# Gathers of 125 edge rows in place of 128 in a three-hop graph kernel

## The reference

```python
edge_index = jnp.stack([src, dst])
h = jnp.maximum(_layernorm(x, axis=-1), 0.0)
head = edge_index[0]; tail = edge_index[1]
rel = edge_emb[edge_type]
agg = entity_emb                      # h
out = jnp.zeros_like(entity_emb)
for _ in range(3):
    h = agg[head]
    t = agg[tail]
    left = h @ q_w
    right = jnp.tanh(rel * t @ k_w)
    att = jnp.sum(left * right, axis=1)
    w = softmax of att over the edges of one head
    msg = w[:, None] * rel * t
    summed = jax.ops.segment_sum(msg, head, num_segments=n)
    agg = summed / jnp.maximum(cnt, 1.0)[:, None]
    norm = jnp.linalg.norm(agg, axis=1, keepdims=True)
    agg = agg / jnp.maximum(norm, 1e-12)
    out = out + agg + entity_emb
x = x + out
```

## Time and profile before

| | |
|---|---|
| median of 3 runs | 2142.53 us |
| lowest, highest | 2138.31, 2146.28 us |
| the profiled execution | 2145.74 us |
| its span, first to last instruction | 2144.0 us |
| POOL, DVE, PE, ACT busy | 1240.4, 1280.6, 1106.5, 843.2 us |
| packets on POOL's DMA queue (q0) | 38400, 72.99 MB |
| packets on SP's DMA queue (q1) | 160708, 228.35 MB |
| TensorE clock granted, mean | 0.684 of full speed |

### The profile page before, as it was taken

One profiled execution on the slowest core, in us unless ns is written; L12 is line 12 of the kernel. 1 busy time (PEld: TensorE's weight loads), 2 busy tenths in 40 slices (PEclk: granted clock), 3 DMA queues, 4 the chain that ended last, 5 costly groups with the idle time before them and its releaser, 6 DMA issues. The chain is left out here.

```text
span 2144.0 us, 22842 instructions
## 1 busy us (share of the span) xinstructions
PE 1106.5 (52%) x5076; PEld 901.9 (42%) x5076; DVE 1280.6 (60%) x5673; ACT 843.2 (39%) x2637; POOL 1240.4 (58%) x1218
## 2 busy tenths in 40 slices
PE   0111355445695545834126668876355479586420
PEld 0001233333584434833114457776344367485310
DVE  8896666566536656178226543845654533788870
ACT  2220566666335565056123311725433312424420
POOL 1003767777557777467777776200177565467776
PEclk9999956665567677555557867856777757755555
DMA  8803455554223343145336645401489865667771
GB/s 228 234 30 124 147 171 165 194 185 150 77 83 108 93 123 112 34 159 172 130 120 202 202 120 136 130 36 66 142 191 158 196 120 135 165 163 201 213 199 34
DMA packets 199245, 302.80 MB, mean 141 GB/s; under 512 B 31284, under 2 KB 113536, under 8 KB 195652
## 3 DMA queue, kind: packets, MB, share of 16 engines
q1 hardware_dynamic: 160708, 228.35, 33.6%
q0 software_dynamic: 38400, 72.99, 16.3%
HBM read 175.78 MB, written 130.86 MB: 143 GB/s over the span
## 5 line engine op out<-in xcount | busy, mean ns | idle before, releaser
L1372 PE MATMUL ps<-rt,wr 128*125 128x128 f32 x1200 | 263.2, 392 | 267.3 <-DVE wr L969 160.3
L574 POOL DMA_INDIRECT tr<-in_x_dram,tidx x200 | 203.4, 1017 | 302.2 <-DVEq L812 184.2
L574 POOL DMA_INDIRECT tr<-agg_d,tidx x200 | 198.9, 995 | 272.1 <-issue 236.8
L1372 PEld LDWEIGHTS ps<-rt,wr 128*125 128x125 f32 x1200 | 233.2, 290 | 290.4 <-DVE wr L969 179.2
L1309 PE MATMUL ps<-ident,rt 128*128 128x128 f32 x600 | 131.2, 358 | 399.2 <-DVE rt L1031 330.7
L1195 ACT ACTIVATE sqj<-ps,invc 125x128 bf16<-125x128 f32 x600 | 214.1, 380 | 291.9 <-PE ps L1372 291.9
L1309 PEld LDWEIGHTS ps<-ident,rt 128*128 128x128 f32 x600 | 91.7, 186 | 424.9 <-DVE rt L1031 349.1
L586 POOL DMA_INDIRECT out_dram<-rt,lidx x200 | 212.2, 1061 | 90.0 <-issue 60.4
L586 POOL DMA_INDIRECT ntab_d<-rt,lidx x200 | 209.2, 1046 | 93.1 <-issue 59.6
L1154 ACT COPY rtT<-ps 128x512 f32<-128x512 f32 x150 | 87.8, 585 | 442.5 <-PE ps L1309 442.5
L1031 DVE TENSOR_TENSOR rt<-tr,relr 128x512 f32<-128x512 f32 x150 | 101.3, 688 | 253.1 <-ACT hr L1146 188.7
(11 more groups left out here) (226 smaller groups left out, 2065.6 us busy)
## 6 DMA issues: line engine op xcount, KB each, us to landing
agg_d<-rt SPq DMA_DIRECT2D x100, 258.0 KB, 2.4
xr<-agg_d SPq DMA_DIRECT2D x100, 258.0 KB, 3.4
relr<-rel_d SPq DMA_DIRECT2D x100, 256.0 KB, 3.6
ntab_d<-rt SPq DMA_DIRECT2D x15, 1679.7 KB
rt<-in_x_dram SPq DMA_DIRECT2D x13, 1024.0 KB, 6.2
out_dram<-rt SPq DMA_DIRECT2D x13, 1024.0 KB, 4.1
acc_d<-xr SPq DMA_DIRECT2D x50, 258.0 KB, 3.2
rel_d<-relr SPq DMA_DIRECT2D x50, 256.0 KB, 2.7
```

Of the source, the lines that this page charges most:

```text
L574: G.indirect_dma_start(out=row, out_offset=None, in_=table[:, :], in_offset=bass.IndirectOffsetOnAxis(ap=idx[:, n:n + 1], axis=0)).then_in ...
L1372: ins = T.matmul(ps[B_T + j % 2][0:R, t, :], wr[:, (j % 2) * GT + t, 0:R], rt[:, j * GT + t, 0:D], start=True, stop=True)
```

## The change

`fetch` reads and writes the first 125 partitions only, in the tile and in the list of row numbers. The three padding partitions of `tr` and `xr` are set to zero once, at the start (from partition 96 on, all rows of the two rings), and no gather writes them again. The scatters and SP's transfers stay as they are.

```diff
             def fetch(row, n, table, idx, done):
-                G.indirect_dma_start(out=row, out_offset=None, in_=table[:, :],
-                                     in_offset=bass.IndirectOffsetOnAxis(ap=idx[:, n:n + 1], axis=0)).then_inc(done, 16)
+                G.indirect_dma_start(out=row[0:R], out_offset=None, in_=table[:, :],
+                                     in_offset=bass.IndirectOffsetOnAxis(ap=idx[0:R, n:n + 1], axis=0)).then_inc(done, 16)
...
             ch.note(V.memset(minus1[:, :], -1.0))
             ch.note(V.memset(onesr[:, :], 1.0))
             ch.note(V.memset(xr[:, :, D:D + 1], 0.0))
+            ch.note(V.memset(tr[96:P, :, :], 0.0))
+            ch.note(V.memset(xr[96:P, :, 0:D], 0.0))
             ch.join()
```

## The result

The changed kernel takes 2234.56 us (median of 4 runs, 2230.95 to 2237.68), the kernel before, measured with it, 2140.42 us (median of 4). The ratio is 1.0439, 95% interval 1.0404 to 1.0474: the change makes the kernel slower by 4.4%, 94 us. The profiled execution has a span of 2230.6 us against 2144.0, so 86.6 us are to be found in the two traces.

What follows compares the result with a forecast made beforehand. Bounds: POOL's cadence early in hop 1, DMA transfers early in hop 2; POOL waits for DVE and ACT in steady hop 0. −0.35 − 2.5 − 1.7 = −4.6 us against the median 2142.53 gives 2138 us; range 2120 to 2190 us.

Steps and rivals of the forecast that it cites:

- part 5 of the change: Spread of a 125-row transfer over DMA engines: 15 engines take 8 rows, one takes 5; 0 us in the sum.
- part 1: POOL's preparation of 800 gathers: 22 ns less each, saving 0.35 us in hop 0 and 2.5 us in hop 1.
- Both signs that the prediction named: POOL's queue and L574: packets other than 32 mean a changed spread; a median over 0.95 us means dearer preparation.
- Its sign for being wrong: Hop 1's first 112 gathers taking more than 140 us; a rising hop 2 share of the DMA engines was another.
- The first rival: Gathers' transfers: five engines take 25 rows each, landing later, cadence unchanged; 2141 to 2144 us, perhaps 2164; chance 0.25.
- The second rival: POOL's preparation at L574, all 800 gathers: uneven gathers dearer; 0.1 us more gives 2158 us, 0.40 gives 2366; chance 0.24.
- Part 2: DMA engines in hop 2: three rows of 128 fewer per gather, saving 1.7 us; nothing in hop 1.
- Part 3: Two settings of zeros on DVE at the start: 2.2 us each, hidden by a 4.49 us wait; 0 us.
- Part 4: Contents of the padding partitions: zero instead of row 0's product, every engine does the same instructions; nothing.
- Reading of the bounds: Stage by stage along POOL's list: where its 1.25 us cadence, its waits for DVE and ACT, or the transfers set time.
- hop 1's first part: First 112 gathers of hop 1, until 1242 us: POOL's cadence is the bound; afterwards POOL waits for DVE, 12.5 us.
- hop 2's first part: Start of hop 2: transfers are late, POOL is ahead; DMA engines 0.93 busy, 11.8 us engine time a gather.

Runs made afterwards that it cites:

- both later measurements: The unchanged change run again beside the kernel before: 2319.74 us against 2471.78 (ratio 0.940), then 2335.95 us against 2517.78 (ratio 0.935).
- the second set: Follow-up kernels beside the kernel before (2529.14 us): one iota per gather 2520.95, 125 rows in hop 1 alone 2476.73, zeros alone 2548.6, spread zero row 2523.71 us.
- the later sets: All follow-up experiments, on four chips, each with the kernel before run beside it, which took 2470 to 2540 us (medians) and not 2140.

## Why the prediction was wrong

**The step that failed** is part 5 of the change, how 125 rows are spread. I took 0 for it, with 15 engines taking 8 rows and one 5, and in part 1 I let POOL's preparation only stay or fall. What the runs showed: a gather's packets are those of 5 engines with 25 rows each, as the row of SP's queue had hinted, and with this spread POOL prepares each of the 800 gathers in 1.210 us and not 0.945, which lengthened the three stages of gathers by 43.6, 39.2 and 17.0 us. I had set the row aside because it was of another queue. Both signs that the prediction named appeared: another number of packets (80 for 32) and a median over 0.95 us at L574. Its sign for being wrong, over 140 us for hop 1's first 112 gathers, could tell nothing: the kernel before took some 146 us for them already (115 in 149.9 us).

The Trainium skill (DMA: Bandwidth & Descriptors, section "Why a DMA increments its semaphore by 16 and not by 1") states that a transfer uses the largest number of engines up to 16 that divides the slowest dimension of both sides, which gives 5 for 125 rows. The packet counts of 112, 124, 125, 126 and 127 rows agree with it on POOL's queue too. I had not used it because its exception for some direct copies of POOL seemed to leave indirect ones open.

**The first rival** had the five engines, but priced only the time to landing. The load of the engines stayed or fell, as it said (POOL's share of the queue row 16.3% before, 13.8% after); it said too that POOL's cadence would stay. That is where the loss is: POOL's preparation grows with the places to fill on all 16 engines.

**The second rival** was right in its place, its price at L574 and its formula. With 0.265 us in it, its terms give (16 x 0.265 − 1.81) x 25 = 61 us in hop 0, 40.5 in hop 1, 17.7 in hop 2; measured 43.6, 39.2 and 17.0. Hop 0's term was too large because POOL's slack there is 62.8 us in all, more than 25 times the 1.81 us of one group: 106 − 62.8 = 43.2. The two times that I gave for this rival, 2158 and 2366 us, are each 1 us more than 2138 + 19 and 2138 + 227. I gave this rival 0.24 and held its price likely to be near 0.1 us; my argument against it, that tables of both row lengths prepare in 0.95 us, said nothing about the number of rows, which no instruction before varied.

**Part 1** (22 ns less a gather, −2.9 us) was wrong in sign and also in kind: of 128 rows to 112 the preparation falls by 12 ns, so three rows less alone would give 2 ns. **Part 2** (−1.7 us on the DMA engines in hop 2) fell away, since POOL became the bound there. But the transfers did get cheaper than expected: POOL's share over 138 us from the first gather of hop 2 fell from 50.9% to 24.9%:

```profile
q0 software_dynamic: 6964, 5.71, 24.9%
```

That is 0.249 x 16 x 138 / 87 = 6.3 us of engine time a gather in place of 11.8, as 6964 packets are 87 gathers. Five engines reading the same row hinder each other less than sixteen, or later than sixteen; the runs don't part the two. **Part 3** was right about each setting (2.2 us worked out, 2.21 and 2.19 measured) and left out the issue before them, so 1.0 us shows at L722, and 0.8 at the first gather. **Part 4** stands: no other engine's work changed by more than 3%.

**Reading of the bounds.** Right for hop 1's first part (POOL) and hop 2's first part (the transfers). With POOL slower by 0.265 us the rest of both hops, where it had waited for DVE, turned POOL-bound too. The scatters' stage after hop 0 gave 10.3 us back: POOL came later to scatters that it had waited for (33.1 us on DVE before, 22.7 after).

**The range** (2120 to 2190) left out 0.10 above; it would have held the result only with a price of the second rival of more than 0.2 us in it.

## What to carry to other kernels

Cutting padding from an indirect DMA of POOL can make POOL's work dearer: 112 or 128 rows cost 0.93 to 0.95 us of POOL, 125 cost 1.21 and 127 cost 2.55. Whether that costs the kernel time depends on who is waited for: the change lost 4.4% where the kernel before took 2140 us, and was 6% faster than it in both later measurements. Count the packets of a gather in the queue's row before a change of shape is thought free, and look up how a number that isn't a multiple of 16 is split. Where a queue's preparation is the cadence of a stage, price a change at it by its number in the stage less the waits that the queue has there.

## What the runs showed of the hardware that I had not expected

- Preparation of an indirect gather: 0.881 us + 0.82 ns x 16 x (rows on one engine) with idle engines, 0.04 us less without; six numbers of rows fit to 0.01 us.
- A gather of hop 2, in which many rows are one row of HBM (over half, by an estimate: 25,000 edges leave at least half of the 50,000 nodes without an outgoing one), takes 10.1 us of engine time, with that row spread over 128 rows 4.1 us, both in the second set.
- In the later sets the kernel before took 2470 to 2540 us, and the change 2320 to 2336, 6% faster than it. Stages in which POOL started a transfer every 1.25 to 1.3 us had grown there by 32 to 151 us, and the change's stages of gathers, at 1.5 us, by at most 4 us. Why is not shown. The measured sign of a change of a few per cent can hang on this; the length of a stage, compared between traces, showed it.
